# Query, key and value projections of an attention kernel on one core: one product over all 128 output columns in place of two products over 64 each

## The reference, cut to what matters

```python
xn = _layernorm(x, axis=-1)
Q = (xn @ Wq).reshape(n, s, 16, 64)      # Wq, Wk, Wv: 128 x 1024
K = (xn @ Wk).reshape(n, s, 16, 64)
V = (xn @ Wv).reshape(n, s, 16, 64)
attn = softmax(einsum('bshe,bthe->bsth', Q, K / sqrt(64)), axis=2)
A = gelu(einsum('bsth,bthe->bshe', attn, V).reshape(n, s, 1024))
s = xn + A @ Wpost
g = silu(_mx_quantize(xn) @ _mx_quantize(weight).T + bias)
out = x + s * g
```

## Time and profile before

| | |
|---|---|
| median of 3 runs | 1539.58 us (1539.15 to 1540.32) |
| the profiled execution's own time | 1540.72 us |
| its span | 1538.9 us |
| TensorE matmul busy | 1461.8 us, 95% |
| TensorE weight load busy | 796.1 us, 52% |
| VectorE busy | 1080.3 us, 70% |
| ScalarE busy | 798.5 us, 52% |
| GpSimd busy | 1151.0 us, 75% |

### The profile page before, as it was taken

The page is one execution under the profiler, slowest core; times in us unless marked ns, Lnnn a source line. Parts: engine busy times, 40 slices in busy tenths (PEclk is TensorE's granted clock), DMA queues, the critical chain, the costliest instruction groups (busy, mean ns, idle before and its releaser), DMA issues. The chain is left out here.

```text
span 1538.9 us, 24806 instructions
## 1 busy us (share of the span) xinstructions
PE 1461.8 (95%) x9857; PEld 796.1 (52%) x9857; DVE 1080.3 (70%) x1408; ACT 798.5 (52%) x1113; POOL 1151.0 (75%) x553
## 2 busy tenths in 40 slices
PE   5999999999999999999999999999999999999387
PEld 3455455555554455555555455555555555555187
DVE  6677777777777777777777777777777777776212
ACT  3455565545545565555445565554555555555253
POOL 0778888887888788778887787788878887789400
PEclk8999999999999999999999999999999999999689
DMA  2000001000000001000000000000000000000396
GB/s 87 1 10 16 16 8 43 17 16 9 16 17 16 8 16 44 16 10 17 16 16 8 16 16 30 10 16 16 16 8 16 17 16 9 17 17 16 122 338 232
DMA packets 43586, 52.12 MB, mean 34 GB/s; under 512 B 2896, under 2 KB 25168, under 8 KB 43472
## 3 DMA queue, kind: packets, MB, share of 16 engines
q1 hardware_dynamic: 42832, 48.44, 9.4%
q0 software_dynamic: 640, 2.10, 0.4%
HBM read 27.46 MB, written 23.07 MB: 33 GB/s over the span
## 5 line engine op out<-in xcount | busy, mean ns | idle before, releaser
L614 POOL TENSOR_TENSOR prob_sum<-prob_sum,probs 128x1024 f32<-128x1024 f32 x384 | 912.0, 2375 | 237.9 <-ACT probs L499 210.4
L726 DVE TENSOR_REDUCE half_maxes<-peaks 128x2 f32<-128x1024 f32 x504 | 611.5, 1213 | 283.8 <-PE peaks L331 282.6
L499 ACT ACTIVATE probs<-scores 128x1024 f32<-128x1024 f32 x512 | 497.1, 1022 | 395.7 <-PE scores L351 395.6
L360 PE MATMUL acc<-probs,vals 128*64 128x512 f32 x2048 | 487.8, 597 | 0.0
L360 PEld LDWEIGHTS acc<-probs,vals 128*64 128x64 f32 x2048 | 137.0, 137 | 246.6 <-issue 218.3
L742 DVE RECIPROCAL inv_sum<-inv_sum 128x128 f32<-128x128 f32 x256 | 240.1, 941 | 10.0 <-ACT inv_sum L483 10.0
L331 PE MATMUL peaks<-k_hi,q_hi 64*128 64x512 f32 x1008 | 225.8, 443 | 0.0
L347 PE MATMUL scores<-q_hi,k_hi 64*128 64x512 f32 x1024 | 202.6, 392 | 0.0
L351 PE MATMUL scores<-max_rows,ones_r 64*128 64x512 f32 x1024 | 201.9, 390 | 0.0
L347 PE MATMUL scores<-q_hi,k_lo 64*128 64x512 f32 x1024 | 201.8, 390 | 0.0
L347 PE MATMUL scores<-q_lo,k_hi 64*128 64x512 f32 x1024 | 201.6, 390 | 0.0
(11 more groups left out here) (112 smaller groups left out, 1001.7 us busy)
## 6 DMA issues: line engine op xcount, KB each, us to landing
att_scratch<-att SPq DMA_DIRECT2D x64, 256.0 KB, 2.0
att_in<-att_scratch SPq DMA_DIRECT2D x32, 512.0 KB, 8.2
xn_scratch<-xn SPq DMA_DIRECT2D x4, 512.0 KB, 3.6
gate_scratch<-gate SPq DMA_DIRECT2D x32, 64.0 KB, 1.5
x_res<-in_L_attn_X SPq DMA_DIRECT2D x8, 256.0 KB, 5.0
xn_res<-xn_scratch SPq DMA_DIRECT2D x8, 256.0 KB, 6.9
out_dram<-res POOLq DMA_DIRECT2D x8, 256.0 KB, 5.8
x_in<-in_L_attn_X SPq DMA_DIRECT2D x3, 512.0 KB, 5.2
```

Source lines behind the costliest of these rows:

```text
L360: last = mm(acc[own[h], :], vals[(s // 2) % 2][:, j, own[h]], probs[j][:, h, :], start=(j == 0), stop=(j == KT - 1), tile_position=col[h])
L499: sa.activation(probs[j][:, :, :], scores[j % 2][:, :, :], ACT.Exp, scale=DH ** -0.5).then_inc(probs_ready, 1)
L614: gp.tensor_tensor(prob_sum[s % 2][:, :, :], before[:, :, :], probs[j][:, :, :], ALU.add).then_inc(probs_summed, 1)
L726: v.tensor_reduce(half_maxes[:, :, f // 2, f % 2], peaks[:, :, :], AX.X, ALU.max).then_inc(peaks_read, 1)
```

## The change

Each pair of products over 64 columns of weights becomes one product over 128 columns, at no tile position. What is computed, into which place of the bank, and the waits ahead of it stay the same. `project` then has 1 product in place of 2, and `project_v` 4 in place of 8.

```diff
@@ project
-                for h in (0, 1):
-                    last = mm(w[own[h], :], weights[:, at + h * DH:at + (h + 1) * DH], xT[n // HP][:, halves[half]],
-                              start=True, stop=True, tile_position=col[h])
-                last.then_inc(filled, 1)
+                mm(w[:, :], weights[:, at:at + P], xT[n // HP][:, halves[half]], start=True, stop=True).then_inc(filled, 1)
@@ project_v
                 for t in range(QT):
-                    for h in (0, 1):
-                        tokens = half * HALF + t * P + h * DH
-                        last = mm(w[own[h], t * P:(t + 1) * P], xT[n // HP][:, tokens:tokens + DH], w_v[:, at:at + P],
-                                  start=True, stop=True, tile_position=col[h])
+                    tokens = half * HALF + t * P
+                    last = mm(w[:, t * P:(t + 1) * P], xT[n // HP][:, tokens:tokens + P], w_v[:, at:at + P], start=True, stop=True)
                 last.then_inc(filled, 1)
```

## The result

The changed kernel takes 1576.79 us (median of 6 runs, 1574.85 to 1580.88), the kernel before, measured beside it, 1538.53 us (median of 6). The ratio is 1.0252, with a 95% interval from 1.0236 to 1.0268: 38.3 us slower, where 38.0 were forecast. The time of 1576.8 lies 0.8 us under the forecast of 1577.6. The six runs lie up to 6 us apart, so a miss this small is finer than they can tell.

A forecast was written before the change was run, and what follows sets the result against it. TensorE was taken as the bound, busy 1303 of 1320 us in the main part. The profiled 1540.72 plus 38.0 gave 1578.7 us; with the runs' median 1.1 us lower, the forecast was 1577.6, range 1566 to 1582.

The forecast's parts named there:

- No streaming is saved: In the projections, one whole-array product streams as long as a pair of column halves, 0.43 us for 512 columns.
- The switch, 0.10 us between any two shapes: Between neighbouring TensorE products, each change among row halves, column halves and whole array costs 0.10 us.
- the rival that ends on the other side: At projections beside `weigh`, halves and whole array are one configuration without drain: 1540 us, not slower; chance 0.03.
- The first load, 0.05 or 0.10 us: Behind a change of shape, the first weight load shows: 0.05 us for a column half, 0.10 for the whole array.
- The rival of the small first load: Projections' first loads behave like the whole-array transposes', 0.05 us cheaper in each of 184 uses: 1568.4 us; chance 0.08.
- The stream of the values: In `project_v`, eight whole-array instructions at 0.112 us replace eight pairs at 0.109, adding 0.02 us a use.
- The rival of the loads that don't hide: In the projections, every whole-array load of 0.10 us shows, not just the first: 1633 us; chance 0.04.
- The count and the cover: Inside the steps, 122 query and key uses by 0.20 and 62 value uses by 0.22 add 38.0 us, nothing hidden.
- The term for the six uses ahead of the steps: Projections before the steps, partly between transposes and partly beside VectorE's reductions: taken as 0, between -0.5 and +0.7 us.
- The wait at the `turn`: TensorE's wait for VectorE's maxima at a step's end hides none of the added time and stays at 16 us.

The follow-up runs named there:

- the single column: Kernel before, plus a whole-array product of one moving column, then overwritten, heading each half-1 query and key projection from pair 1 on: 1567.06 us, ratio 1.0192.
- the same column in halves: Kernel before, plus a product of one moving column, split into two column halves, heading the same half-1 query and key projections: 1547.45 us, ratio 1.0064.
- The `ffn` run: Kernel before, with the whole-array product `ffn` between a peak and `weigh` made into two column halves: 1533.46 us, ratio 0.9973.
- The mix of shapes: Kernel before, with the values' tiles 0 and 2 as whole-array products and tiles 1 and 3 left as column halves: 1580.61 us, ratio 1.0276.

## Why the prediction was right

*No streaming is saved.* Right: the second MATMUL of a whole-array projection lasts 592 ns as before, and of the projection's 1.06 us 0.86 are left for streaming when the switch and the first load are taken off.

*The switch, 0.10 us between any two shapes.* Right in all four directions that the change uses: from a peak into the whole array it is the 0.32 us between starts that it was into column halves, and the other three are in the distances above. The point that the rows before left open, a plain whole-array product directly behind column halves, measures 0.10 (1.81 us for `weigh` with the single column behind it, 1.72 with the same column in halves). With that the rival that ends on the other side, in which column halves and the whole array are one configuration, is out. The Trainium skill, page "TensorEngine Tiling (Array Packing)", section "Key Properties", says that a change of tiling mode drains the engine and a change of the tile alone doesn't. The two runs with one column more agree with that: 0.10 us at the change of shape, none between column halves.

*The first load, 0.05 or 0.10 us.* Right: 697 against 592 ns. The rival of the small first load, read off the transposes, would have had 0.05 here. Why a whole-array float32 transpose loads 128 columns in 0.140 us and a product in 0.190 was not tried.

*The stream of the values.* Right: 1.09 us and 378 against 276 ns. The rival of the loads that don't hide is out; only the first of eight shows. The Trainium skill, page "TensorE: Matmul & The Clock Gate", section "Part 3: Packing small matmuls — row/col tiling", says that a load overlaps running products only where row groups differ. This stream doesn't agree: its loads of about 0.19 us use the same rows as the products that hide them, and eight products take 1.09 us.

*The count and the cover.* 122 uses by 0.20 and 62 by 0.22 were 24.4 and 13.6; alone they measure 24.2 and 14.2. Added up over all pairs of the changed kernel's trace, the uses and `weigh` take 37.4 us more; the other 1.2 of the 38.6 us is spread over peaks and scores, and no run shows its cause. That the total agrees with the forecast to 0.3 us is therefore partly luck; the prices themselves are right to about 0.01 us a use. The term for the six uses ahead of the steps, put at 0 between -0.5 and +0.7 us, can't be tested to that fineness by these runs. The wait at the `turn` covered nothing, since VectorE's chain to it starts from a peak in the same round, and the projections are rounds ahead. The `ffn` run shows the other case: an edit in the round of the `turn` did meet that wait, by 1.1 us.

Some sizes of the experiments were a little off. The mix of shapes cost 42.0 us against 39, for the reason given there. The extra column in halves cost 9.8 us against 7 to 9, with only two runs; its trace has 0.11 us for each of 62 uses, 6.8 us, so some 3 us of it are not shown to come from the edit. The gain at `ffn` was put at 6.2 in place of 4.2: the sum left out the wait right behind it, which was named only as a rival and explains 1.1 of the 2.0 us.

## What to carry to other kernels

Two products on the column halves of the array already run at the same time, so merging them into one saves instructions and no time; what a product costs beyond its stream depended in these runs on the shape of its neighbours. Count the places at which the shape changes, in this kernel (its three shapes, at a granted clock of 1.00) at 0.10 us for each and 0.05 or 0.10 us for the load that shows behind it, and give a short product the shape of what stands around it, even if that takes more instructions. Look for that price in distances between starts: busy time puts it inside the products, and the page shows no wait for it. What the price is for other shapes or types of data, no run here shows.

## What I had not expected

That the wait at the `turn` would take back the whole gain of `ffn` in some rounds and none in the others: 0.20 us longer in six rounds, untouched in the other 25.

Two more sizes were forecast from the prices but may still surprise a reader. A whole-array product of a single moving column, between column halves, costs 0.46 us, more than half of a projection of 512 columns (0.86). And the mix of both shapes in one use was the slowest kernel of all: 42 us over the kernel before, 28 us over the one with the same values as whole-array products.
